# A hyena and FFN layer on one core: the usual one of two TensorE program bodies is placed where a branch falls through

## The reference

```python
xn = layernorm(x)                          # x: 1 x 4096 x 256
# branch 1: hyena
h    = layernorm(xn) * gamma + beta
proj = h @ W_in + b_in                     # three parts v, g0, g1 of 256 channels
y = v
for kern, g in ((k0, g0), (k1, g1)):       # 128 taps for each channel
    y = causal_conv(y, kern) * g
attn = xn + y @ W_out + b_out
# branch 2: gated FFN, integer weights scaled by 1/127
ffn = (silu(xn @ w_gate.T) * (xn @ w_up.T)) @ w_down.T     # 768 hidden
out = x + attn + ffn
```

## Time and profile before

| | |
|---|---|
| median of 3 runs | 351.94 us (351.06 to 352.59) |
| the profiled execution | 351.36 us |
| its span, first to last instruction | 349.5 us |
| busy share of PE, DVE, POOL, ACT | 88%, 71%, 62%, 52% |
| mean granted clock of TensorE | 0.974 |
| matmuls on PE | 4941 |

### The profile page before, as it was taken

The page is one execution under the profiler, slowest core; times in us unless marked ns, Lnnn a source line. Parts: engine busy times, 40 slices in busy tenths (PEclk is TensorE's granted clock), DMA queues, the critical chain, the costliest instruction groups (busy, mean ns, idle before and its releaser), DMA issues.

```text
span 349.5 us, 11796 instructions
## 1 busy us (share of the span) xinstructions
PE 307.8 (88%) x4941; PEld 239.7 (69%) x4941; DVE 247.0 (71%) x498; ACT 181.8 (52%) x379; POOL 215.7 (62%) x302
## 2 busy tenths in 40 slices
PE   0767777776897999999999999999999999998995
PEld 0355666655775777777777777777777876657994
DVE  3996983555357577568567678867766966897895
ACT  3634886954335354443444444434544344549992
POOL 3979999302887888866876776777886782210000
PEclk9965998999999999999999999999999999999999
DMA  7990260006687957879578687786786969400445
GB/s 236 349 357 21 70 235 4 0 9 232 241 311 255 388 194 308 314 250 387 206 304 345 249 366 247 288 356 229 333 304 262 381 240 344 169 0 2 164 140 180
DMA packets 21506, 81.01 MB, mean 232 GB/s; under 512 B 1479, under 2 KB 12619, under 8 KB 13259
## 3 DMA queue, kind: packets, MB, share of 16 engines
q1 hardware_dynamic: 19458, 77.47, 59.3%
q0 software_dynamic: 1840, 2.36, 3.1%
q10 hardware_dynamic: 152, 0.40, 0.4%
HBM read 75.50 MB, written 4.72 MB: 229 GB/s over the span
## 4 chain that ended last, share of the span: by engine, by line
PE 44%; DVE 17%; POOL 15%; ACT 12%; issue 7%; DMA 2%; SPq 0%; POOLq 0%; DVEq 0%; ACTq 0%
PE bank_c L282 11%; PE bank_p L282 8%; PE bank_u L282 8%; PE bank_g L282 8%; PE bank_d L282 8%; ACT vx L734 3%; DVE hhl L934 3%; ACT vx L726 3%; POOL ybuf L1136 3%; DVE sgh L929 2%; DMA res<-in_L_attn_x 2%; POOL ybuf L1240 2%; POOL res L1187 2%; ACT hhl L664 2%; POOL res L1188 2%
## 5 line engine op out<-in xcount | busy, mean ns | idle before, releaser
L282 PE MATMUL bank_d<-wd,hhl 128*128 128x256 f16 x384 | 84.3, 271 | 0.3 <-DVE hhl L934 0.2
L282 PEld LDWEIGHTS bank_p<-wq,xT 128*128 128x128 f16 x1536 | 71.4, 99 | 14.5 <-issue 0.3
L282 PE MATMUL bank_p<-wq,xT 128*128 128x64 f16 x1536 | 80.6, 194 | 0.2 <-issue 0.2
L282 PE MATMUL bank_u<-xT,wgu 128*128 128x512 f16 x192 | 66.2, 378 | 0.4 <-DVE sgh L929 0.4
L282 PE MATMUL bank_g<-xT,wgu 128*128 128x512 f16 x192 | 66.2, 377 | 0.0
L282 PEld LDWEIGHTS bank_c<-ybuf,bands 128*128 128x128 f16 x1024 | 51.4, 96 | 21.2 <-issue 4.5
L282 PE MATMUL bank_c<-ybuf,bands 128*128 128x64 f16 (+3 forms) x1024 | 60.2, 184 | 3.8 <-DVE ybuf L954 3.8
L282 PEld LDWEIGHTS bank_c<-vhl,bands 128*128 128x128 f16 x1024 | 49.0, 96 | 18.5 <-issue 3.1
L282 PE MATMUL bank_c<-vhl,bands 128*128 128x64 f16 (+3 forms) x1024 | 57.3, 184 | 2.1 <-DVE x1y L788 0.9
L664 ACT CAST hhl<-sgh 128x512 f16<-128x512 f32 x48 | 29.7, 619 | 47.2 <-DVE sgh L929 47.2
L1144 POOL TENSOR_TENSOR vx<-vx,bias 128x512 f32<-128x512 f32 x32 | 37.8, 1184 | 25.2 <-DVE vx L796 25.2
(11 more groups left out here) (177 smaller groups left out, 557.3 us busy)
## 6 DMA issues: line engine op xcount, KB each, us to landing
bands<-taps_seq SPq DMA_DIRECT2D x64, 1024.0 KB, 8.1
out<-res SPq DMA_DIRECT2D x8, 512.0 KB, 2.9
res<-in_L_attn_x SPq DMA_DIRECT2D x3, 1024.0 KB, 10.9
res<-in_L_attn_x SPq DMA_DIRECT2D x2, 512.0 KB, 6.2
bands<-in_L_attn_W_in SPq DMA_DIRECT2D x1, 768.0 KB, 6.2
bands<-in_L_ffn_w_gate POOLq DMA_DIRECT2D x1, 768.0 KB, 7.3
bands<-in_L_ffn_w_up POOLq DMA_DIRECT2D x1, 768.0 KB, 8.8
vx<-in_L_ffn_w_down POOLq DMA_DIRECT2D x1, 768.0 KB, 9.9
```

The lines of the kernel that those rows point to most:

```text
L282: return nc.tensor.matmul(o, w, m, start=start, stop=stop, skip_group_check=True)
```

## The change

Three things are written differently, all in PE's program.

- The condition is turned round, `general < 1`, and with it the order of the two bodies: `body(False)` is the part of the `If`, `body(True)` that of the `Else`.
- The loop of the last stage (`transpose_y(b)`, `project_out(b - 2)`) moves from behind the branch into `body`, so it exists in both bodies.
- `project_out` is therefore defined ahead of the branch.

```diff
                 transpose_y(1)
                 for i in range(8):
                     down_part(STEPS - 1, i, general)
+                for b in range(2, NB + 2):
+                    if b < NB:
+                        transpose_y(b)
+                    project_out(b - 2)
...
-            pe.wait_ge(flag_ready, 1)
-            general = pe.value_load(flag[0:1, 0:1], min_val=0, max_val=1)
-            with pe.If(general > 0):
-                body(True)
-            with pe.Else():
-                body(False)
...
-            for b in range(2, NB + 2):
-                if b < NB:
-                    transpose_y(b)
-                project_out(b - 2)
+            for b in range(FORK):
+                first_stage(b)
+
+            pe.wait_ge(flag_ready, 1)
+            general = pe.value_load(flag[0:1, 0:1], min_val=0, max_val=1)
+
+            with pe.If(general < 1):
+                body(False)
+            with pe.Else():
+                body(True)
```

More of the change, by code:

```diff
@@ L547, in transpose_y @@
                 last.then_inc(y_tp, 1)
-            for b in range(FORK):
-                first_stage(b)
-            pe.wait_ge(flag_ready, 1)
-            general = pe.value_load(flag[0:1, 0:1], min_val=0, max_val=1)
-            with pe.If(general > 0):
-                body(True)
-            with pe.Else():
-                body(False)
             def project_out(b):
```

## The result

| | before | changed |
|---|---|---|
| median | 352.59 us (350.18 to 354.16, 11 runs) | 349.80 us (349.42 to 351.66, 11 runs) |
| profiled execution | 351.36 us | 349.42 us |
| its span | 349.5 us | 347.5 us |

The ratio over all these executions is 0.994, with a 95% interval of 0.9911 to 0.9969. By it the change makes the kernel 0.6% faster, 2.1 us of 352 (the two medians lie 2.8 us apart); 0.7% was forecast, and the range held the time. The median of before is 0.65 us above the one that the forecast started from, since more runs now stand behind it.

A forecast was written before the change was run, and what follows sets the result against it. PE was taken to pace the main loop, with the gain in its gap at the fork, which delays ACT and the weight pairs. Only that shift counted, -2.5 us, other terms 0: 351.94 - 2.5 = 349.4 us, range 348.4 to 351.2.

The forecast's parts named there:

- The branch falls through: PE's fork after block 21: the branch falls from 3.36 to about 0.1 us, removing PE's 2.76 us idle time.
- ACT, and POOL next: First stage, blocks 22 to 26: ACT starts earlier until POOL's normalising limits it; block 26 at 59.3, a 2.5 us shift.
- The clock: PE's clock behind the fork's gap: the drop to 1.2 GHz probably doesn't come there; nothing counted for it.
- Pairs and main loop carry it through: Weight pairs start 2.5 us earlier, at 63.9, and the main loop passes the whole -2.5 us on.
- The near jump: Jump at the end of the usual body to the row behind it, now gone: 0.1 us gain at most, 0 taken.
- the last stage twice: Last stage's copy in body(True): same instructions run, the program is only longer; 0 us.
- The jump at PE's end, cost 0: New jump over body(True) at PE's end: takes 3.36 us, hidden while SP waits for the last output write; cost 0.
- the cover of 1.1: End of program: 1.1 us remaining between the end of PE's 3.36 us jump and SP reaching the barrier.
- that the jump sticks out at the end: Rival, program end: output writes delay the jump's fetch, making PE last; 351.2 us, or 352.7 and slower; chance 0.11.
- The branch that costs the same when it falls through: Rival at the fork: falling through still costs 3.36 us, nothing gained, 351.9 us; chance 0.07.
- The gain lost on the way: Rival, after the fork: later blocks, DVE, POOL or code packets take back half the gain, 350.7 us; chance 0.08.

The follow-up runs named there:

- near jump: The kernel before with body(True) replaced by an already fulfilled wait, so the taken branch's target is two rows on; median 348.25 us, ratio 0.9863-0.9933.
- scales' move: The changed kernel with POOL's second scales of the last batch moved from its step 23 to step 27; medians 349.09 and, repeated, 349.08 us.
- fork only: The kernel before with only the order of the two bodies turned round, the last stage staying behind the branch; median 352.66 us, ratio 1.0001-1.0063.
- stage only: The kernel before with the last stage written into both bodies, their order unchanged; median 352.92 us, ratio 1.0002-1.0073.
- two kernels without a far jump: The kernel before with body(True) replaced by a fulfilled wait, 348.25 us, and the changed kernel without its Else part, 348.18 us.
- tail of two: The changed kernel with POOL's second scales at step 27 and SP's last four-block write issued as two writes of two blocks; median 348.84 us.
- changed again: The changed kernel repeated without any edit; median 350.04 us, ratio to before 0.9907-0.9965.
- no end jump: The changed kernel with its Else part, body(True), left out, so PE's end has no far jump; median 348.18 us, ratio to before 0.9861-0.9928.
- scales before: The kernel before with POOL's second scales of the last batch moved from its step 23 to step 27; median 351.71 us, ratio 0.9968-1.0032.

## Why the prediction was right, and where not

1. *The branch falls through.* Right: 86 ns, for which 0.1 us was taken, and PE without idle time between blocks 21 and 22. The near jump adds that the distance, and not the taking, is what costs.
2. *ACT, and POOL next.* Right in place and size: block 26 at 59.15 (59.3 forecast), the pair at 63.77 (63.9). The pair's shift is 2.68 us, of which 0.14 already stood between the two executions ahead of the fork; 2.54 are left for the 2.5 of the forecast. The scales' move shows that POOL was the limit.
3. *The clock.* Right for this execution, with full clock from 52 us on. But the step took it for a matter of the gap alone. PE now waits 1.72 us before block 26, and in near jump and fork only the clock was at 1.2 GHz behind this wait and the pair came at 64.9 and 64.6. The cost was there to be named.
4. *Pairs and main loop carry it through.* Right, and 0.34 us more came at one matmul at 161.4 us, where the kernel before stood on "issue".
5. and 6. *The near jump, and the last stage twice.* The near jump was put at nothing, and no run gives it more. That the second copy costs nothing wasn't confirmed: stage only came out 0.9 us slower in the median, and in its profile PE stood 1.34 us at a code packet behind the branch. The step left out that the copy moves the code against the packets.
7. *The jump at PE's end, cost 0.* **This term was mis-sized.** The row of the fork's jump (3.36 us) was taken for one beside the output's writes; it takes 4.5 to 4.6 us there. Even so it ended 1.0 us ahead of SP, nearly the cover of 1.1. The cost came on the other side. The step asked only what the writes do to the fetch, and not what the fetch does to the last write, which SP waits for: 1.1 us. In the profiled pair PE's last matmul came 3.24 us earlier: 0.14 from ahead of the fork, 2.54 from the fork, 0.34 from the main loop's stall and some 0.2 in small steps. With 1.1 to 1.2 us given back at the end, 2.0 us are left, for a forecast of 2.5. That it came so near is in part luck: without the 0.7 us from outside the forecast's steps, 1.3 would be left.

Of the rivals, that the jump sticks out at the end named the right place, and had the wrong one of the two waiting. The branch that costs the same when it falls through is refuted. The gain lost on the way was in part what happened in other executions: by the clock behind block 26.

The two kernels without a far jump stand at 348.2 in the median, 1.6 to 1.9 us under the change. The last write explains 1.1 us of that; the remainder, 0.2 to 0.5 us by the ratios to before, is open and within the intervals.

## What to carry to other kernels

Here a branch over the other body, some 3,000 rows, cost PE 3.3 to 3.6 us wherever nothing else held up its fetch, and a fall-through or a short jump 0.1 to 0.25 us; so lay out the likely path as the one that falls through, and carry it to the end of the program, since turning the order alone only moves the jump. Put the far jump where the engine has nothing left to do, and ask also what its fetch of code does to the transfers that others wait for at that moment. When a stall of one engine goes, look at once for the work of another that it covered: here POOL's power was worth 1.0 us of ACT's time with the gap gone, and nothing before.

Of the kernels that still have both bodies, the change with POOL's scales moved comes to 349.08 us, 0.8% under before (0.9884 to 0.9948), for 0.6% with the change alone. The tail of two on top of it has the lowest median, 348.84, but can't be told from it.

## What had not been expected of the hardware

Executions of one kernel differ in when code packets arrive. In the changed kernel's repetition PE stands in the main loop, at a matmul without any wait of its own:

```profile
270.77 0.38 PE L282 MATMUL bank_g<-xT,wgu 128*128 128x512 f16 x1
271.79 0.34 PE L282 MATMUL bank_p<-wq,xT 128*128 128x64 f16 x6 [0.64 <-issue]
```

The same matmul came without delay in the first profile of this kernel, where a packet of the instruction queue began between 264 and 266 us. In the repetition no packet began there; one did between 269.3 and 269.5, 2.4 us ahead of the stalled matmul. Four of the profiles (changed again, near jump, no end jump, fork only) lost 0.5 to 0.8 us at this one place. Other profiles stood in the same way at other matmuls: stage only at 58.0 and 107.6 us, scales before 0.54 us at 259.9, the kernel before at 161.4. The matmul that ended each of these stalls came 2.2 to 2.7 us after a packet began, as at the fork before (packet at 52.3, matmul at 54.85). So PE is held up where a packet begins less than that ahead of need. Why the packet begins late in some executions no run here shows. The clock is the other part of the scatter: TensorE was at 1.2 GHz for some microseconds at 48, at 55, at 57 or at 60 us, each time behind a wait of PE in the first stage or shortly after one, and not in every execution of the same waits.
